# Moving the feed-forward output of a phase-mixer layer from ScalarE and an accumulating DMA to VectorE

## What is computed

```python
x = x + mixer(layernorm(x))      # mixer(x) returns x + h
x = x + ffn(layernorm(x))

# mixer: phases are a cumulative sum over the sequence
phi = cumsum((x @ W_omega.T + b_omega) * exp(log_scale) / sqrt(position))
cm_real, cm_imag = x * cos(phi), x * sin(phi)
mem_real, mem_imag = cumsum(cm_real) / position, cumsum(cm_imag) / position
ret_real = mem_real * cos(phi) + mem_imag * sin(phi)
ret_imag = mem_imag * cos(phi) - mem_real * sin(phi)
context = concat(cm_real, cm_imag, ret_real, ret_imag)        # 1024 wide
h = gelu(layernorm_affine(context) @ W1.T + b1) @ W2.T + b2   # 512 hidden

# ffn: weights quantised to -1, 0, 1
out = relu(x @ Wq1.T + b1) @ Wq2.T + b2                       # 1024 hidden
```

## Time and profile before

| | before |
|---|---|
| median of the runs | 1550.1 us |
| the profiled execution's own time | 1550.92 us |
| its span, first to last instruction | 1549.1 us |
| TensorE busy (matmuls) | 95% |
| VectorE busy | 91% |
| ScalarE busy | 81% |
| GpSimd busy | 40% |
| granted TensorE clock, mean | 0.992 |

### The profile page before, as it was taken

The page is one execution under the profiler, slowest core; times in us unless marked ns, Lnnn a source line. Parts: engine busy times, 40 slices in busy tenths (PEclk is TensorE's granted clock), DMA queues, the critical chain, the costliest instruction groups (busy, mean ns, idle before and its releaser), DMA issues.

```text
span 1549.1 us, 29929 instructions
## 1 busy us (share of the span) xinstructions
PE 1467.3 (95%) x10685; PEld 880.1 (57%) x10685; DVE 1416.0 (91%) x2324; ACT 1257.5 (81%) x1773; POOL 623.2 (40%) x394
## 2 busy tenths in 40 slices
PE   3779999999999999999999999999999999999998
PEld 2445566565556656556656555665655665555566
DVE  6989999999999999999999999999999999999854
ACT  6758888889888888988888988888898888898756
POOL 1423544433444434354443344443335444344331
PEclk9899999999999999999999999999999999999999
DMA  6325355556545555645655654555564555565452
GB/s 217 69 55 110 71 99 110 104 110 123 101 78 110 104 108 117 114 88 91 111 103 109 123 96 83 109 106 108 115 119 79 97 110 103 109 123 96 70 95 42
DMA packets 231427, 158.20 MB, mean 102 GB/s; under 512 B 138608, under 2 KB 221552, under 8 KB 231280
## 3 DMA queue, kind: packets, MB, share of 16 engines
q0 software_dynamic: 59376, 83.37, 32.9%
q1 hardware_dynamic: 170272, 69.25, 19.0%
q10 hardware_dynamic: 1632, 3.67, 0.6%
HBM read 24.13 MB, written 33.03 MB: 37 GB/s over the span
## 4 chain that ended last, share of the span: by engine, by line
PE 75%; DVE 10%; issue 5%; ACT 5%; POOL 1%; DMA 1%; SPq 1%; DVEq 0%; ACTq 0%; POOLq 0%
PE ps L962 37%; PE ps L996 12%; PE ps L1017 10%; PE ps L983 7%; PE ps L922 5%; PE ps L935 3%; DVE rr L1315 2%; DVE arena L1393 2%; ACT arena L705 2%; ACT arena L714 1%; PE ps L948 1%; DVE arena L1325 1%; POOL sqr L535 1%; POOL sqr L537 1%; SPq L438 1%
## 5 line engine op out<-in xcount | busy, mean ns | idle before, releaser
L962 PE MATMUL ps<-arena,w_hi 128*128 128x512 f16 x2048 | 609.0, 379 | 3.8 <-DVE arena L1325 1.9
L962 PE MATMUL ps<-arena,w_lo 128*128 128x512 f16 x1024 | 388.1, 379 | 0.0
L962 PEld LDWEIGHTS ps<-arena,w_hi 128*128 128x128 f16 x2048 | 197.9, 98 | 224.5 <-issue 2.4
L996 PE MATMUL ps<-fw_t,arena 128*128 128x256 f16 x2048 | 254.8, 272 | 27.2 <-DVE arena L1393 27.2
L996 PEld LDWEIGHTS ps<-fw_t,arena 128*128 128x128 f16 x2048 | 197.9, 98 | 92.0 <-issue 46.5
L983 PE MATMUL ps<-turned,fw_t 128*128 128x512 f16 x1024 | 247.3, 379 | 1.2 <-DVE arena L1349 0.6
L705 ACT ACTIVATE arena<-ps,relu_bias,relu_scale 128x512 f32<-128x512 f32 x256 | 197.6, 772 | 34.7 <-PE ps L983 34.6
L535 POOL TENSOR_TENSOR sqr<-sqr,turn 128x1024 f32<-128x1024 f32 x32 | 83.7, 2617 | 339.1 <-DVE arena L1325 339.1
L1393 DVE TENSOR_TENSOR arena<-arena 128x512 f16<-128x512 f32 x256 | 173.0, 686 | 29.8 <-ACT arena L714 29.7
L1017 PE MATMUL ps<-w_hi,arena 128*128 128x256 f16 x1024 | 172.9, 273 | 0.3 <-issue 0.3
L962 PEld LDWEIGHTS ps<-arena,w_lo 128*128 128x128 f16 x1024 | 100.1, 98 | 120.8
(11 more groups left out here) (188 smaller groups left out, 2827.3 us busy)
## 6 DMA issues: line engine op xcount, KB each, us to landing
x_rows<-in_L_attn_x SPq DMA_DIRECT2D x32, 512.0 KB, 4.7
rr<-qa POOLq DMA_DIRECT2D x32, 512.0 KB, 7.5
ri<-qb POOLq DMA_DIRECT2D x32, 512.0 KB, 9.1
base<-bias_rows POOLq DMA_DIRECT2D x32, 512.0 KB, 5.5
x<-bias_rows POOLq DMA_DIRECT2D x32, 512.0 KB, 5.8
out<-x SPq DMA_DIRECT2D x31, 512.0 KB, 9.8
out<-x POOLq DMA_DIRECT2D x31, 512.0 KB, 12.0
arena<-in_L_attn_W ACTq DMA_DIRECT2D x1, 2048.0 KB, 11.3
```

Source lines behind the costliest of these rows:

```text
L962: last = pe.matmul(ps[:, 4 + m], w[:, k, m * P:(m + 1) * P], a[:, c.b, k], start=(i == 0), stop=(i == len(passes) - 1))
L996: last = pe.matmul(ps_rows_a[:, j], a[:, m % SLOTS, j * P:(j + 1) * P], fw2_t[:, m], start=(m == 0 and j % 2 == 0 and a is rh), stop=(m == ...
```

## The change

- VectorE gets `output(c)`: x1 = down * PSUM + x1 in one instruction over the whole chunk. It stands behind `second_lo(now)` in a usual step, behind `second_lo(now)` and ahead of `context_variance` in the step of the last mixer, and ahead of the first `relu_lo` in the last step. The two-part output of the last chunk is now called `last_output`.
- ScalarE's `output`, GpSimd's `output_sum` and the semaphores `added` go. `out` is written once a chunk: SP's store moves from chunk `now`, where it waited for the bias, to chunk `before`, where it waits for `out_done`. It keeps its place in SP's order, behind the transposes and the load of x.
- `mixer_residual` waits for that store instead of for the addition.
- On VectorE `relu_lo(now, 1)` stands ahead of `product_real_sin(ahead)` instead of behind it. `relu_lo(now, 0)` already stood ahead of the retrieval product before it.

```diff
@@ sync
-                if (c := s.chunk(0)) and c.index < CHUNKS - 1:
-                    need_dma(sp, x1_biased, c)
+                if c := s.chunk(-1):
+                    need(sp, out_done, c)
                     sp.dma_start(out_v[c.index], x1[:, c.b]).then_inc(stored[c.b], 16)
@@ gpsimd
-            def output_sum(c):
-                need(pool, out_done, c)
-                pool.dma_start(out_v[c.index], x1[:, c.b], accum_op=ALU.add).then_inc(added[c.b], 16)
...
-                if before:
-                    output_sum(before)
@@ scalar
-            def output(c):
-                need_block(act, f2_done, KF - 1, c)
-                need(act, xs2_done, c)
-                need_dma(act, stored, c)
-                act.activation(x1[:, c.b], ps_rows_a, ACT.Copy, scale=down[:, 4:5]).then_inc(out_done, 1)
...
-                if before:
-                    output(before)
@@ vector
-                need_dma(dve, added, c, 2)
+                need_dma(dve, stored, c, 2)
...
             def output(c):
                 need_block(dve, f2_done, KF - 1, c)
                 need_dma(dve, x1_biased, c)
+                dve.scalar_tensor_tensor(out=x1[:, c.b], in0=ps_rows_a, scalar=down[:, 4:5], in1=x1[:, c.b],
+                                         op0=ALU.mult, op1=ALU.add).then_inc(out_done, 1)
...
                 if now:
                     second_lo(now)
+                if before:
+                    output(before)
                 if ahead:
                     memory_imag(ahead)
...
+                if now:
+                    relu_lo(now, 1)
                 if ahead:
                     product_real_sin(ahead)
-                if now:
-                    relu_lo(now, 1)
```

More of the change, by code:

```diff
@@ L247, in phase_mixer_layer @@
         stored = [sem(f"stored{i}") for i in range(2)]
-        added = [sem(f"added{i}") for i in range(2)]
         base_biased = [sem(f"base_biased{i}") for i in range(2)]
@@ L461, in _ @@
             sp.wait_ge(stored[0], 16 * (CHUNKS // 2))
-            sp.wait_ge(added[0], 16 * (CHUNKS // 2))
             sp.wait_ge(stored[1], 16 * (CHUNKS // 2 + 1))
-            sp.wait_ge(added[1], 16 * (CHUNKS // 2 - 1))
         @block.gpsimd
@@ L509, in step @@
             def step(s):
-                before, now, nxt, ahead, far = s.chunk(-1), s.chunk(0), s.chunk(1), s.chunk(2), s.chunk(3)
+                now, nxt, ahead, far = s.chunk(0), s.chunk(1), s.chunk(2), s.chunk(3)
                 if ahead:
@@ L714, in relu_hi, with last_mixer @@
                 act.copy(rh[:, m % SLOTS], rf[:, m % SLOTS]).then_inc(rh_done, 1)
-            def last_mixer(before, now, last):
+            def last_mixer(now, last):
                 sums_hi(last)
-                output(before)
                 normalise_2(now)
@@ L738, in step @@
             def step(s):
-                before, now, nxt, ahead, far = s.chunk(-1), s.chunk(0), s.chunk(1), s.chunk(2), s.chunk(3)
+                now, nxt, ahead, far = s.chunk(0), s.chunk(1), s.chunk(2), s.chunk(3)
                 if now and not ahead:
                     if nxt:
-                        last_mixer(before, now, nxt)
+                        last_mixer(now, nxt)
                     else:
-                        output(before)
                         for m in range(KF):
@@ L1398, in output, with last_output @@
                 need_dma(dve, x1_biased, c)
+                dve.scalar_tensor_tensor(out=x1[:, c.b], in0=ps_rows_a, scalar=down[:, 4:5], in1=x1[:, c.b],
+                                         op0=ALU.mult, op1=ALU.add).then_inc(out_done, 1)
+            def last_output(c):
+                need_block(dve, f2_done, KF - 1, c)
+                need_dma(dve, x1_biased, c)
                 for half in range(2):
@@ L1402, in output, with last_mixer @@
                                              in1=to, op0=ALU.mult, op1=ALU.add).then_inc(out_done, 1)
-            def last_mixer(now, last):
+            def last_mixer(before, now, last):
                 lean_2(now)
                 second_lo(now)
+                output(before)
                 context_variance(last)
@@ L1424, in step @@
             def step(s):
-                now, nxt, ahead, far = s.chunk(0), s.chunk(1), s.chunk(2), s.chunk(3)
+                before, now, nxt, ahead, far = s.chunk(-1), s.chunk(0), s.chunk(1), s.chunk(2), s.chunk(3)
                 if now and not ahead:
                     if nxt:
-                        last_mixer(now, nxt)
+                        last_mixer(before, now, nxt)
                     else:
+                        output(before)
                         for m in range(KF):
                             relu_lo(now, m)
-                        output(now)
+                        last_output(now)
                     return
```

## The result

The changed kernel takes 1564.0 us (median of 4 runs, 1561.47 to 1569.58) against 1550.62 for the kernel before beside it; the ratio is 1.0093, with a 95% interval of 1.0062 to 1.0124. It is slower by some 13 us, as forecast (1563.6). The profiled execution took 1561.47 us with a span of 1559.7, 10.6 more than before.

What follows compares the result with a forecast made beforehand. TensorE's circle with its badly placed low half bounded the kernel, VectorE's 45.15 us circle next; 45.15 + 1.20 - 0.14 = 46.21 us over 28 periods, +13.1, plus ri's 0.4: +13.5, 1563.6 us, range 1554 to 1570.

Steps and rivals of the forecast that it cites:

- VectorE's circle: VectorE from `fraction` to the last context low half, back through GpSimd and ScalarE: 45.15 us, 46.21 after the change.
- Output 1.20 us: VectorE's new output instruction, wholly inside its closed circle of waits, lengthens each step by 1.20 us.
- Way back shorter by 0.14: Return through GpSimd and ScalarE to `fraction`: scans queued earlier shorten GpSimd's second addition, taking 0.14 us off each step.
- ri's transfer, 0.4 us: DMA of ri, later because qb comes 0.61 us later, delays VectorE's last context low half: 0.4 us in all.
- TensorE would wait ahead of the first output matmuls, for the low half: TensorE, ahead of the first feed-forward output matmuls: waits 1.3 us a step for VectorE's first relu low half.
- ScalarE and GpSimd gain nothing: Output leaving ScalarE and accumulating DMA leaving GpSimd: 0 gained, since the sine waits longer and GpSimd stood idle.
- (a): Dearer return through GpSimd and ScalarE: scans give nothing back, ri late every step; +19.8 us, 1570; chance 0.16.
- (b): Cheaper return: GpSimd's first addition back at 2.34 us; +4.7 us, 1554.8; chance 0.09.
- (c): Faster: return more than 0.6 us shorter, TensorE's circle decides, its removed stop pays; -11 us, 1539; chance 0.05.
- (d): The change's two halves cancel: return through GpSimd and ScalarE shorter by 0.6 us; 1550 us; chance 0.05.
- TensorE's 44.87: TensorE's own closed circle: 44.87 us of work a step, its 0.86 us stop for the second low half excluded.
- (e): VectorE saturated: the output's full 1.20 us a step comes out as time; +33.6 us, 1584; chance 0.03.

Runs made afterwards that it cites:

- output_early: The changed kernel with VectorE's output at the head of the step, ahead of `fraction`, instead of behind the second layer's low half: 1552.8 us, ratio 1.0015.
- output_twice: The changed kernel with VectorE computing the output twice, first into a spare tile nobody reads, in all chunks but the last three: 1597.61 us, ratio 1.0301.
- stats_first: The changed kernel with the second layer's statistics ahead of the phase scans, the output left where the change put it: 1542.71 us, ratio 0.9955.
- after_again: The changed kernel as it is, run again beside the run before it on one chip: 1563.08 us (1560.39 to 1567.57).
- lo_only: The kernel before with only the second relu low half moved ahead of the product qb: 1538.04 us, ratio 0.9913.
- before_lo_stats: The kernel before, output on ScalarE and accumulating DMA kept, with the low half moved and the statistics ahead of the scans: 1525.68 us, ratio 0.9838.
- early_stats: The changed kernel with both the output ahead of `fraction` and the second layer's statistics ahead of the phase scans: 1526.09 us, ratio 0.9841.

## Why the prediction was right

The sum: forecast 28 periods of 46.21 and +13.5 us; measured regular periods of 46.16 and 46.00 us, 46.08 on average, and +13.4 by the medians. The mechanism was right, but that the two sums agree so closely is luck. The regular steps give 28 x 46.08 = 1290.2 us against 1280.8 before, so +9.4 where the forecast had +13.1: its period was 0.13 too long. Lengthened steps, for which the sum had no term, make up for it: 1.6 us of them in the profiled execution, the fastest of the four, whose span is 10.6 us longer than before; the median run is 2.5 us above that execution.

- *VectorE's circle decides, by the way back through GpSimd and ScalarE.* Right, and shown from three sides: the place of the output (`output_early`), its doubling (`output_twice`) and the shorter way back (`stats_first`) each moved the regular steps by what the circle gives. By the medians that holds for the doubling (33.6 us) and the shorter way back (21); the early output gained 11, where its regular steps give 28 x (46.08 - 45.52) = 16.
- *Output 1.20 us.* Measured 1.19. But VectorE's outward part grew by 1.09 only, from 36.33 (36.89 - 0.47 and 36.94 - 0.70, averaged) to 37.42. Of the missing 0.10, 0.08 is a term that I had not seen. A line of the kernel before, the one ahead of the wait of 0.47:

```profile
735.00 0.68 DVE L1349 TENSOR_TENSOR arena<-ps,rb 128x512 f32<-128x512 f32 x1
```

  There 0.68 us pass until the idle time begins (736.15 - 0.47), against 0.60 after the change (740.68 to 741.28): instructions overlap by 0.08 when the next one is ready, and a wait loses this too. A wait removed gives back a little more than its listed length.
- *Way back shorter by 0.14.* Right: 8.66 in both parities against a mean of 8.82, so 0.16, with L526 at 2.64 as it was left, and L528 at 2.06.
- *ri's transfer, 0.4 us.* Hardly seen: VectorE waits 0.26 ahead of L1306 in one step (46.71 us). ScalarE does wait longer for it (37.9 us in 30 waits, 9.0 in 14 before), but its copy is still in time. rr now lands 5.8 us after its issue (7.5 before) and ri 8.7 (9.1 before), with the accumulating stores gone.
- *TensorE would wait ahead of the first output matmuls, for the low half.* The size was right, the place wrong. It waits ahead of the input matmuls of block 3 (741.42, 1.13 us, for L1330), because they overwrite the PSUM bank of the hidden block that VectorE scales there. I had followed only the low halves. It cost nothing, since TensorE had this time to wait anyway.
- *ScalarE and GpSimd gain nothing.* Right: the sine waits 40.1 us in 31 waits instead, and GpSimd 11.41 instead of 10.68 ahead of L526.
- *The lengthened steps.* Not in the sum. The first profiled execution has some 1.6 us of them, the second (`after_again`) some 9. The runs spread from 1560 to 1570, where those of the kernel before lie within 2.7 us.
- The rivals: (a) and (b) were the bounds of the way back and fell with 8.66; (c) and (d) needed a way back shorter by 0.6 or more, which the change doesn't bring and `stats_first` does. Rival (c) was also mislabelled: at 0.6 shorter the change only breaks even, and its 45.35 is still VectorE's circle; TensorE's 44.87 would decide from 46.35 - 44.87 = 1.48 on. In `stats_first` the way back is 0.96 shorter, and VectorE's circle still decides. Rival (e), the saturated VectorE, falls with `output_early`, and holds only from the point where the room is used up (`output_twice`).

What stays open: with the statistics first, the gain of `lo_only` rises from 12 to 25 us where the regular circles explain some 3 of the difference. That VectorE's 0.7 us of slack then swallows most of the late steps is argued from the traces, not shown by an experiment of its own.

## What to carry to other kernels

In a pipeline of many engines, look for closed circles of waits from one instruction to itself a step later, and sum each with its waits taken out; the share of busy time says neither which circle is the longest nor how much room there is. Idle time of an engine is room only if it lies on the engine's circle, not beside a way back through others, and a gain on one circle stays hidden until the others are as short. Where VectorE and GpSimd have to run side by side, put VectorE's work with a PSUM operand or a single input next to GpSimd's, and its two-operand SBUF work elsewhere; that order alone was worth 21 us in the changed kernel, and nothing in the kernel before, where TensorE's circle was the longer one.

## What the runs showed of the hardware

- GpSimd's addition of 512 columns lasts 1.27 us beside statistics and 2.06 to 2.26 beside VectorE's scans. Two scans last 2.45 us by themselves, 3.36 beside one addition, and 4.18 when they are there before the first addition ends, in an early step 4.62. Whoever is second stands.
- A transposing DMA usually lands 2.5 us after its issue. In the step above one took 6.9, and TensorE did not only lose the wait: its granted clock was 0.50, the lower of its two levels (1.2 GHz), for the next 5.3 us, after 3.44 us without a matmul. The stretch with the stop at its end and the one behind it (us; then each engine's busy time, the granted clock, the DMA share and GB/s):

```profile
300.00:332.80 32.80, 28.27 (x204) 14.50 (x202) 30.10 (x57) 29.69 (x44) 13.46 (x9) 0.99 0.53 90
332.90:338.20 5.30, 5.30 (x14) 1.94 (x15) 5.30 (x7) 0.89 (x1) 0.00 (x0) 0.50 0.90 235
```

- The clock fell at shorter stops too. In `output_twice` TensorE stands for 2.3 to 2.5 us in 20 of the steps, ahead of the input matmuls, and around the end of eight of these stops (from 0.4 us ahead of it to 1.3 behind) its granted clock fell to 0.50 for 3.4 us; in the changed kernel it stands for 1.1 to 1.6 us a step and the clock stays at full speed through all 28. The first of the eight:

```profile
188.83 1.04 PE L965 MATMUL ps<-turned,fw_t 128*128 128x512 f16 x4 [2.50 <-DVE arena L1331]
...
190.98 1.91 PE L965 MATMUL ps<-turned,fw_t 128*128 128x512 f16 x4
```

  It cost nothing there, since TensorE had the time to spare.
- Leaving out the accumulating stores took 16 MB off the traffic to memory. With TensorE's circle deciding, the kernel with them (`before_lo_stats`, 1525.68 us) and the one without (`early_stats`, 1526.09 us) are equally fast.
